# A first stage pipelined one batch deeper, and the order of a head-attention step, in a four-layer graph network

## The reference

```python
# layer 0
x = x * node_weights[None, :, None] + node_bias[None, :, None] + x
h = jnp.einsum('bnf,fo->bno', x, W)
h = (h - mu) * rsqrt(var + LN_EPS) * ln_gamma + ln_beta
s1 = h @ a1
s2 = h @ a2
e = leaky_relu(s1[:, :, None] + s2[:, None, :], 0.2)
attention = softmax(where(adj > 0, e, NEG_INF))
h = elu(einsum('bij,bjo->bio', attention, h) + h)
# layer 1, 4 heads of 32
scores = einsum('bhnd,bhmd->bhnm', q, k) / sqrt(32)
attn = softmax(where(adj == 0, -inf, scores))
# layer 2
deg = jnp.sum(mask, axis=-1)
agg = einsum('ij,bjf->bif', mask, x) / maximum(deg, 1.0)
```

## Time and profile before

| | |
|---|---|
| median of 3 runs | 4012.62 us (4012.45 to 4014.85) |
| the profiled execution | 4011.27 us, span 4009.7 us, mean granted PE clock 0.925 |
| PE busy | 3619.6 us (90%) |
| DVE busy | 3105.6 us (77%) |
| ACT busy | 1737.6 us (43%) |
| POOL busy | 1850.5 us (46%) |
| stage 0 | 0 to 295.7 us |
| head attention, its loop | 1008.4 to 2968 us |

### The profile page before, as it was taken

The page is one execution under the profiler, slowest core; times in us unless marked ns, Lnnn a source line. Parts: engine busy times, 40 slices in busy tenths (PEclk is TensorE's granted clock), DMA queues, the critical chain, the costliest instruction groups (busy, mean ns, idle before and its releaser), DMA issues. The chain is left out here.

```text
span 4009.7 us, 70877 instructions
## 1 busy us (share of the span) xinstructions
PE 3619.6 (90%) x21004; PEld 1881.2 (47%) x21004; DVE 3105.6 (77%) x7153; ACT 1737.6 (43%) x3560; POOL 1850.5 (46%) x853
## 2 busy tenths in 40 slices
PE   6758999774999999999999999999978799889999
PEld 4538999752111111111111111111116589789999
DVE  6657888766898989989899898998967645467777
ACT  5541111072565656656566565665634423310000
POOL 1110000010788888888888888888853201100000
PEclk7669999996899999999999999999987799989999
DMA  5412122156011000101101010000025444221211
GB/s 193 162 68 86 70 81 85 45 221 222 4 28 27 26 24 9 26 27 26 28 5 26 27 28 27 18 15 27 26 67 201 188 159 157 105 84 71 80 56 51
DMA packets 66869, 288.70 MB, mean 72 GB/s; under 512 B 12482, under 2 KB 14916, under 8 KB 47044
## 3 DMA queue, kind: packets, MB, share of 16 engines
q1 hardware_dynamic: 64228, 267.55, 19.2%
q0 software_dynamic: 2304, 16.84, 1.0%
HBM read 174.12 MB, written 110.23 MB: 71 GB/s over the span
## 5 line engine op out<-in xcount | busy, mean ns | idle before, releaser
L1266 POOL TENSOR_TENSOR a_w<-a_w,keep_mask_t 128x1024 f32<-128x1024 f32 x768 | 1683.4, 2216 | 368.9 <-ACT a_w L1253 368.9
L1202 DVE CUSTOM_DVE_ANT_0 a_mx_ps<-a_mx_ps,a_mbias 128x512 f32<-128x512 f32 x2112 | 1403.2, 718 | 226.1 <-PE a_mx_ps L1128 202.2
L1253 ACT ACTIVATE a_w<-a_sc_ps 128x512 f32<-128x512 f32 x2048 | 1111.4, 595 | 823.0 <-PE a_sc_ps L1165 821.6
L1144 PE MATMUL a_o_ps<-a_w,a_v 128*33 128x512 f32 x4096 | 1086.0, 610 | 4.7 <-POOL a_w L1266 4.7
L778 PE MATMUL g_acc<-g_hv,g_w 128*128 128x129 f32 x8192 | 927.5, 277 | 41.1 <-ACT g_hv L736 24.9
L778 PEld LDWEIGHTS g_acc<-g_hv,g_w 128*128 128x128 f32 x8192 | 925.2, 193 | 43.6 <-DVE g_w L715 37.3
L715 DVE SCALAR_TENSOR_TENSOR g_w<-g_row,keep_s,keep_mask_t 128x1024 f32<-128x1024 f32 x512 | 647.4, 1283 | 211.2 <-PE g_acc L778 191.8
L1165 PE MATMUL a_sc_ps<-a_qs,a_ks 97*128 97x512 f16 x2048 | 636.4, 393 | 26.3 <-issue 26.0
L1165 PEld LDWEIGHTS a_sc_ps<-a_qs,a_ks 97*128 97x128 f16 x2048 | 118.8, 97 | 847.7 <-ACT a_w L1253 796.4
L1128 PE MATMUL a_mx_ps<-a_ks,a_qs 32*128 32x512 f16 x2112 | 423.7, 398 | 51.7 <-DVE a_mx L1202 32.9
L1128 PEld LDWEIGHTS a_mx_ps<-a_ks,a_qs 32*128 32x128 f16 x2112 | 99.7, 91 | 537.2 <-issue 412.7
(11 more groups left out here) (168 smaller groups left out, 2394.1 us busy)
## 6 DMA issues: line engine op xcount, KB each, us to landing
p_x<-x SPq DMA_DIRECT2D x24, 1024.0 KB, 8.3
g_h<-h_nodes SPq DMA_DIRECT2D x16, 1032.0 KB, 6.1
p_adj_in<-in_adj SPq DMA_DIRECT2D x16, 1024.0 KB, 7.2
g_row<-u_rows SPq DMA_DIRECT2D x32, 512.0 KB, 7.5
a_v<-v SPq DMA_DIRECT2D x18, 528.0 KB, 3.7
a_ks<-k_hi SPq DMA_DIRECT2D x72, 128.0 KB, 2.7
a_qs<-q_hi SPq DMA_DIRECT2D x72, 128.0 KB, 3.0
v<-p_v SPq DMA_DIRECT2D x8, 1056.0 KB, 6.8
```

The lines of the kernel that those rows point to most:

```text
L1144: mm = nc.tensor.matmul(o_ps[2 * HD * a:2 * HD * a + HD + 1, c % 2, :], v[u][:, jt, a, :], w[:, g % PB, a, :], start=(jt == 0), stop=(jt = ...
L1202: last = nc.vector.tensor_tensor_reduce(out=mx_ps[:, buf, a, :], in0=mx_ps[:, buf, a, :], in1=mbias[:, t, kc * BANK:(kc + 1) * BANK], scal ...
L1253: nc.scalar.activation(w[:, g % PB, a], sc_ps[:, n % SB], ACT.Exp, scale=SCALE).then_inc(exp_done, 1)
L1266: nc.gpsimd.tensor_tensor(w[:, g % PB], w[:, g % PB], keep["mask_t"][:, jt, c * BANK:(c + 1) * BANK].unsqueeze(1).to_broadcast([P, 2, BANK ...
```

## The change

**In stage 0**

- `hn` and `h0` get a second buffer, and each engine's turn a new list. ACT takes `norm_x` of batch b + 1 in four pieces between the copies of batch b, and `norm_h` of batch b - 1 at the end. DVE takes `stats_h`, `scores` and `affine` of batch b - 1 and `stats_x` of batch b + 2. The masks stay at b + 1. `rstd_x` and `shift_x` are still single: `root_x(b + 2)` waits until ACT has normed all of batch b + 1. A last `stats_h`, `scores`, `affine` and `norm_h` follow the loop. On SP the load of x(b + 3) waits for the same semaphore and now stands ahead of the loads of `adj`.
- The node bias is split into three bfloat16 parts (`split_nb`, 8 small DVE operations), which are summed in the matmul, so that `nb_spread` and `ones` are bfloat16 with 96 rows where they were float32 with 16.
- `mask` no longer sums the rows. At the end of the stage PE counts the degree from `mask_t` in 256 matmuls of one output column, and DVE makes `has_deg` and `rdeg` there, no longer in `row_shifts`.
- Ahead of the first turn `stats_x(1)`, `split_nb` and `mask(0, 1)` now stand before `prepare`, and the load of x(1) before that of the second slab and the small weights.

**In head attention** the first `slot` of a step is moved ahead of its two score matmuls.

```diff
-        hn = s.sb("hn", [P, T, F])
+        hn = [s.sb(f"hn{k}", [P, T, F]) for k in range(2)]
         hT = s.sb("hT", [P, N])
-        h0 = s.sb("h0", [P, T, E])
+        h0 = [s.sb(f"h0{k}", [P, T, E]) for k in range(2)]
...
-        nb_rows = s.sb("nb_rows", [T, P])
-        nb_spread = s.sb("nb_spread", [T, T, P])
-        ones = s.sb("ones", [T, P])
+        nb_left = s.sb("nb_left", [P, T])
+        nb_part = s.sb("nb_part", [P, 2, T], BF16)
+        nb_parts = s.sb("nb_parts", [P, 3, 32])
+        nb_rows = s.sb("nb_rows", [96, P])
+        tile_of = s.sb("tile_of", [96, T])
+        nb_spread = s.sb("nb_spread", [96, T, P], BF16)
+        ones = s.sb("ones", [P, P], BF16)
+        deg = s.sb("deg", [P, T])
...
-            def following(b, k):
-                sp.wait_ge(x_normed, b + 1)
-                load_x(b + 2, k)
+            def load_masks(b):
                 for a in range(2):
-                    sp.wait_ge(m01_ready, 2 * (b + 1) + a + 1)
-                    load_adj(b + 2, a)
-                    store_mbias(b + 1, a)
+                    sp.wait_ge(m01_ready, 2 * (b - 1) + a + 1)
+                    load_adj(b, a)
+                    store_mbias(b - 1, a)
+            def turn(b, k, half):
+                if not isinstance(b, int) or b < B - 3:
+                    sp.wait_ge(x_normed, CH * (b + 2))
+                    load_x(b + 3, 1 - k)
+                if not late(b):
+                    load_masks(b + 2)
+                if not first(b):
+                    store_h(b - 1)
...
             def root_x(b):
-                pool.wait_ge(x_normed, b)
+                pool.wait_ge(x_normed, CH * b)
...
             def turn(b, k, half):
-                if not last(b):
-                    root_x(b + 1)
-                root_h(b)
+                if not first(b):
+                    root_h(b - 1)
+                if not late(b):
+                    root_x(b + 2)
...
-                                        adj_in[:, k, :].rearrange("p (q t) -> p t q", t=T), 0, 0.0, ALU.is_gt, ALU.add,
-                                        accum_out=keep["rdeg"][:, bass.ds(2 * b + k, 1)]).then_inc(m01_ready, 1)
+                                        adj_in[:, k, :].rearrange("p (q t) -> p t q", t=T), 0, None, ALU.is_gt).then_inc(m01_ready, 1)
...
             def turn(b, k, half):
+                if not first(b):
+                    stats_h(b - 1, 1 - k)
                 if not last(b):
                     mask(b + 1, 0)
-                    stats_x(b + 1, 1 - k, half + k)
-                stats_h(b)
+                if not late(b):
+                    stats_x(b + 2, k, half + 1)
                 if not last(b):
-                    shift_of_x(b + 1)
                     mask(b + 1, 1)
-                scores(b)
+                if not first(b):
+                    scores(b - 1, 1 - k)
+                if not late(b):
+                    shift_of_x(b + 2)
                 if not first(b):
                     affine(b - 1)
             stats_x(0, 0, 0)
             mask(0, 0)
             shift_of_x(0)
+            stats_x(1, 1, 0)
+            split_nb()
+            mask(0, 1)
             prepare()
-            mask(0, 1)
+            shift_of_x(1)
             batches(dve, turn)
+            stats_h(B - 1, 1)
+            scores(B - 1, 1)
             affine(B - 1)
+            dve.wait_ge(counted, 1)
+            nc.vector.tensor_scalar(keep["has_deg"][:], pj_ps[:, 0, 0:T], 0.0, None, ALU.is_gt)
+            nc.vector.tensor_scalar(deg[:], pj_ps[:, 0, 0:T], 1.0, None, ALU.max).then_inc(counted, 1)
+            dve.wait_ge(counted, 2)
+            nc.vector.reciprocal(keep["rdeg"][:], deg[:])
...
             def turn(b, k, half):
-                keep_nodes(b)
+                def ahead(q):
+                    if not last(b):
+                        norm_x(b + 1, 1 - k, q)
+                if not first(b):
+                    act.wait_ge(scores_kept, 2 * (b - 1))
+                keep_hT(b, 0)
+                keep_hT(b, 1)
+                ahead(0)
+                keep_h0(b, k, 0)
+                keep_h0(b, k, 1)
+                keep_hT(b, 2)
+                ahead(1)
+                keep_h0(b, k, 2)
+                keep_hT(b, 3)
+                ahead(2)
+                keep_h0(b, k, 3)
                 keep_mask(b, 0)
+                keep_h0(b, k, 4)
+                ahead(3)
+                keep_h0(b, k, 5)
                 keep_mask(b, 1)
-                if not last(b):
-                    norm_x(b + 1, 1 - k)
-                norm_h(b)
+                if not first(b):
+                    norm_h(b - 1, 1 - k)
...
-            def turn_nodes(b, q):
+            def turn_nodes(b, k, q):
+                pe.wait_ge(x_normed, CH * b + q + 1)
                 pe.wait_ge(hT_kept, CH * b + q + 1)
-                nc.tensor.matmul(tp_ps[:, q % 2, :], ones[:], nb_spread[:, 4 * q:4 * q + 4, :].rearrange("k t p -> k (t p)"),
+                nc.tensor.matmul(tp_ps[:, q % 2, :], ones[0:96, :], nb_spread[:, 4 * q:4 * q + 4, :].rearrange("k t p -> k (t p)"),
                                  start=True, stop=False, skip_group_check=True)
...
+            pe.wait_ge(mt_kept, 2 * B + 2)
+            pe.wait_ge(h0_kept, TH * B + 2)
+            for it in range(T):
+                for jt in range(T):
+                    mm = nc.tensor.matmul(pj_ps[:, 0, it:it + 1], keep["mask_t"][:, jt, it * P:(it + 1) * P], ones[:, 0:1],
+                                          start=(jt == 0), stop=(jt == T - 1))
+            mm.then_inc(counted, 1)
...
-                    if jt == 0:
-                        pe.wait_ge(shift_placed, 32 * (CHUNKS * i + g // T + 1))
-                    for a in range(2):
-                        n = 2 * g + a
-                        pe.wait_ge(exp_done, 2 * BODY * i + (n + 1 if n else SB))
-                        nc.tensor.matmul(sc_ps[:, n % SB, :], ks[u][a][:, jt * P:(jt + 1) * P],
-                                         qs[u][a][:, c * BANK:(c + 1) * BANK], start=True, stop=True).then_inc(scored, 1)
                     on, tu, tc = target(g // T)
                     if jt == 0 and tc == 0:
                         pe.wait_ge(qk_loaded[tu], LOADS * (i + on + 1))
                     mine_now = of_step(jt)
                     slot(mine_now[0], CHUNKS * i + g // T + 2, tu, tc)
+                    if jt == 0:
+                        pe.wait_ge(shift_placed, 32 * (CHUNKS * i + g // T + 1))
+                    for a in range(2):
+                        n = 2 * g + a
+                        pe.wait_ge(exp_done, 2 * BODY * i + (n + 1 if n else SB))
+                        nc.tensor.matmul(sc_ps[:, n % SB, :], ks[u][a][:, jt * P:(jt + 1) * P],
+                                         qs[u][a][:, c * BANK:(c + 1) * BANK], start=True, stop=True).then_inc(scored, 1)
                     if g >= LAG:
                         weigh(g - LAG, i)
```

142 lines of the change are left out of this document (74 added, 68 removed).

## The result

| | before | changed kernel |
|---|---|---|
| median of the runs | 4012.53 us (4006.11 to 4014.85) | 3907.78 us (3904.39 to 3912.55) |
| profiled execution, its span | 4011.27, 4009.7 us | 3912.55, 3910.8 us |
| mean granted clock | 0.925 | 0.939 |

The ratio is 0.9742, with a 95% interval of 0.9725 to 0.9759. The direction held and the size did not. Two executions further down, one of e3 (5101.22 us) and one of e5 (4021.83 us), fell into a slower state of the chip and are left out of every median and ratio.

What follows compares the result with a forecast made beforehand. The prediction had a ring through PE, ACT and DVE pace stage 0, and PE pace head attention. Stage 0 -63, counting +1 and head attention +3 gave -59 us on 4011.27, so 3952, with 1.35 for the median 3953; range 3918 to 3987.

Steps and rivals of the forecast that it cites:

- I take 3.60, the row with the same reads: Stage 0, DVE: the mask without its row sum would still take 3.60 us, within bounds of 0.69 and 3.60.
- The fast mask: Rival, stage 0: plain mask takes half of 3.60, clock high, ACT sets the pace at 21 us; 3933 us, chance 0.18.
- I take the middle, 24 us per batch: Stage 0 loop: 24 us per batch, between 22 at the high clock and 26 at the low one.
- Head attention, +3: Head attention: steps stay 1.84 us; scores coming 0.32 later at 8 batch ends, and the loop's start, cost 3 us more.
- The low clock: Rival, stage 0: PE's clock stays low, so 26 us per batch; 3972 us in all, chance 0.2.
- The new wait: Rival, stage 0: waiting for the shift of b + 2 costs DVE 5 us per batch; 3983 us, chance 0.1.
- The ring of row maxima: Rival, head attention: late DVE masks stall PE in 256 steps, at 0.3 us each +77; 4030 us, chance 0.05.
- scores to weighted sum at 0.43: Rival, head attention: this part of each step costs 0.43 us, not 0.54, 112 us less; 3841 us, chance 0.05.
- S: Theory set up after the measurement, stage 0: its extra gain comes from the plain mask.
- P: Theory set up after the measurement, stage 0: extra gain comes from ACT setting the pace, DVE's work mattering little.
- H: Theory set up after the measurement, head attention: its gain is due to the order of the groups.
- C: Theory set up after the measurement: some gain comes from where PE's later code now lies, not the change itself.

Runs made afterwards that it cites:

- e3: Changed kernel, but each stage 0 mask operation keeps its row sum: 3911.87 us, 0.9769 of the kernel before.
- e5: Changed kernel with the mask's row sum kept and the bias in float32, leaving stage 0's deeper pipelining: 3946.79 us, 0.9856 of the kernel before.
- e6: Kernel before plus only the plain mask and the degree counted on PE: 4004.17 us, 0.9988 of the kernel before.
- e4: Changed kernel with the bias product in float32 again, still on 96 rows: 3942.92 us, 0.9846 of the kernel before.
- e12: Changed kernel, but PE makes the tenth step's pair of row maxima right behind the ninth's: 3968.04 us, 0.9893 of the kernel before.
- e1: Kernel before plus only the reordered step of head attention: 3999.84 us, 0.9971 of the kernel before.
- e8: Kernel before plus 374 idle one-column products at the end of stage 0's PE program: 4001.26 us, 0.9985 of the kernel before.
- e7: Changed kernel plus 24 idle one-column products at the end of stage 0's PE program: 3930.25 us, 0.9801 of the kernel before.
- e10: Changed kernel, but DVE instead of ACT scales the last 8 of 16 norm_h tiles: 3895.31 us, 0.9712 of the kernel before.
- e9: Changed kernel, but DVE instead of ACT scales the last 4 of 16 norm_h tiles: 3901.61 us, 0.9729 of the kernel before.
- e2: Changed kernel with the scores first again in head attention, so only stage 0 is changed: 3916.86 us, 0.9764 of the kernel before.
- e11: e10 with both masks of a turn ahead of stats_x: 3895.67 us, 0.9712 of the kernel before.

## Why the prediction was wrong

**What bounded the kernel: right.** The ring through PE, ACT and DVE was the pace of stage 0. e5 shows that breaking it gives 57 us, and e6 that 3.4 us less DVE work in each turn gave nothing measurable while it stood.

**"I take 3.60, the row with the same reads": wrong, a term mis-sized.** The plain mask took 1.90. My bounds of 0.69 and 3.60 held it, but I placed it at the wrong end. The reads were the same; the row sum made the difference, as e3 shows by bringing 3.64 back. The fast mask was a rival at 0.18, with half of 3.60, ACT at the pace and 21 us per turn, and its working is very near what happened in stage 0: 21 per turn and -83 there, against 21.7 and -80.5. It was worth 8.2 us of the 46 that I missed, not most of it. Of the two rules weighed in the prediction, neither gives 1.90. The 1227 ns of the Trainium skill's perf-mode tier table (VectorE: DVE Perf Modes) is given for float32 and says nothing of strides; this strided int32 form measured 0.67 us more; the penalty for each new 16-byte line (SBUF — State Buffer, Door 1) did not keep the operation at 3.60.

**"I take the middle, 24 us per batch": wrong, a term mis-sized.** With the mask at 3.60, as I had it, e3 measured 23.0: near the 22 that I had worked out for the high clock. Two terms were off. DVE's list was 20.6 us and not the 21.7 that I had added up. And the clock rose from 0.63 to 0.77, where I had argued that PE's similar busy share would leave it where it was. The busy share did stay similar (71%, and in e5 73%), and the clock rose all the same (0.77, and in e5 0.79), so that argument was the wrong step. The rise came with the broken ring, since e5 has it without the other two parts; what in the new order raised it stays open. Six turns of 1.0 are 6 us, the start is 2.2 better than forecast (`stats_h` at 47.8 instead of 50), the end 0.8 (33.2 instead of 34): with e3, stage 0 ends at 218.9 and not 228.

**The bias: right.** I had a product of 0.27 at the high clock and some 0.5 at the low; it was 0.22 and 0.43. e4 put 14.6 us on its float32 form.

**The count, 17 to 30 us: wrong, and without cost.** I priced a load and a one-column product like a turn of a slab with 128 columns, 0.066 to 0.118. They take 0.027. The cover would have held either way but for the 1 us I charged.

**Head attention, +3: wrong, a step that was not looked at.** The steady step came out as worked, 1.84, with scores to weighted sum at 0.53 to 0.54. But I took "each group costs the same whatever follows" from one steady step and never laid out the joint, where the transpose stands in a pair's place: 7 us of gain in 64 joints. Why the joint is cheaper is not shown (see e12). POOL's 0.32 at a batch's end was 0.13 (a wait of 0.72 instead of 0.59), and the start of a turn was not longer. e1 gives 11.6 us less (7.6 to 16) in place of my 3 more. Of the 12 us in the two traces, 3.7 are the long first turn of the one trace of before, which is no gain of the order.

**What I had not asked at all: where later code lies.** I put the rest of the program at nothing. 8 us of g3 belong to no part of the edit's own work, and e8 gets 7 of them with idle instructions. The same thing could have gone against the change: 24 products more, and 22 us would have been lost (e7).

**The rivals.** The low clock did not stay. The new wait exists, 1.62 us of DVE for POOL's root in a turn, as the plain mask holds the root up; it is hidden, since ACT sets the pace (e10 fills it with DVE's tiles, and `affine` waits for ACT in the changed kernel). The ring of row maxima did not stall: PE's idle time for DVE's maxima is 33.4 us after and 32.9 before in the page. But e12 shows the price of asking 1.5 us earlier. No step shows scores to weighted sum at 0.43.

Of the four theories, S accounts for 8.2 us of stage 0. P holds as to the pace (e9, e10), though 3.4 us more of DVE's work did cost 1.25 in a turn (e3). H holds for the joints (e1, e2), and C for g3 (e8).

In sum: against 39.7 us missed in the profiled executions, stage 0 holds 18.5 (8.2 the mask, 9 the clock, start and end, 1 the count), head attention 15 (7 the joints, 3 that I had charged, 5 the first turn of the loop), code placement 8, and the rest of the program takes back 1.8. The other 6 of the 46 in the medians are that the profiled execution of the changed kernel was the slowest of its four, 4.8 above the median, while that of before was 1.3 below.

## What to carry to other kernels

When a ring is broken, price each engine's list in full and take the pace from the fullest, then ask what the clock does when the stalls go; a work item that was free inside the ring gets its price only afterwards (the plain mask: nothing measurable in the old order, 8 us in the new). Lay out a reordered step at its exceptions too, its joints and turns, and not just once in the steady state. And before an effect of under 1% in a kernel with long unrolled loops is credited to an edit, compare the stages that were not edited: here idle instructions alone moved the whole time by 9 us one way and 22 the other.

## What the runs showed that I had not expected

- PE stops for 0.7 to 4.2 us at the turns of loops, each time until 1.2 to 1.9 us after a packet of instructions has come in. Whether a stop is there depends on how much code lies ahead: 48 instructions more added a second stop of 2.4 to 3.7 us in seven turns of the head loop, and the low clock at the start of these turns lasted 10 to 14 us instead of 7 to 10 (a head loop of 1966.3 instead of 1947.4).
- A comparison of strided int32 to bfloat16 on 128 x 2048 elements takes 1.90 us on DVE plain and 3.60 with a row sum.
- POOL's power of 128 x 16 elements, 2.90 us, takes 4.4 to 4.7 when it starts just behind the plain mask on DVE, that is 1.5 to 1.8 longer, a little less than the mask's 1.90. Beside the mask with its sum it takes 2.90 (e3). In e11 the root for the shift, which there runs beside no mask, is back at 2.90, and the other one, with two plain masks beside it, takes 4.6 to 5.2. The Trainium skill (SBUF — State Buffer, Who interferes with whom) describes a pair of ports that POOL and DVE hold one at a time, and says that the plain `tensor_scalar` can take it and the form that also writes its accumulator does not. Both halves of that agree with these numbers.
- In head attention DVE's products of weights and mask rose from a mean of 1373 to 1798 ns by the page, and POOL's fell from 2216 to 2155, though neither was edited. That they meet at other times since the scores come 0.32 us later in the step was only argued; with PE setting the pace it cost nothing.
- A 128-column bfloat16 weight load with a one-column product has a pitch of 27 ns, 256 of them in 6.9 us, at a mean clock of 0.57.
